# Attention with routed experts on one core: values and first sums of a group at step 5, and the low part of the row maxima between the two maxima of that step

## The reference

```python
x = x + attention(layernorm(x), ctx)          # kv = ctx @ Wkv.T, q = ln(x) @ Wq.T, causal softmax, @ Wout.T
x = x + ffn(layernorm(x))
# ffn: logits (T, 512, 8); probs = softmax; top 2 of 8, weights divided by their sum
#      final[t,o] = sum_e c[t,e] * (h @ expert_w[e].T + expert_b[e])[t,o]
#      with c[t,e] = sum over o of the weight that column o gives to e
```

## Time and profile before

| | |
|---|---|
| runs of the kernel before | 1996.59 us median of 3 (1994.41 to 1997.58) |
| the profiled execution, its own time | 1992.97 us |
| span of its profile | 1991.2 us |
| TensorE clock granted, whole span | 0.991 |
| PE busy | 1910.7 us, 96% |
| DVE busy | 1432.4 us, 72% |
| ACT busy | 1038.7 us, 52% |
| POOL busy | 858.1 us, 43% |
| chain that ended last, PE's share | 62% |

### The profile page before, as it was taken

The page is one execution under the profiler, slowest core; times in us unless marked ns, Lnnn a source line. Parts: engine busy times, 40 slices in busy tenths (PEclk is TensorE's granted clock), DMA queues, the critical chain, the costliest instruction groups (busy, mean ns, idle before and its releaser), DMA issues.

```text
span 1991.2 us, 30425 instructions
## 1 busy us (share of the span) xinstructions
PE 1910.7 (96%) x9772; PEld 1512.0 (76%) x9772; DVE 1432.4 (72%) x2840; ACT 1038.7 (52%) x2062; POOL 858.1 (43%) x1016
## 2 busy tenths in 40 slices
PE   4899999999997899999999999999999999999999
PEld 3666777777764788888888888788888888888887
DVE  5667767767666848787888888477777777777732
ACT  2566566566554347877777877533444333344400
POOL 5577777777676235455454435101321111132100
PEclk8999999999998999999999999999999999999999
DMA  5554555455465477786856455732232222223111
GB/s 165 122 127 127 134 143 134 123 143 138 106 176 197 158 243 239 242 269 222 253 211 232 168 207 195 285 111 79 82 125 89 79 87 92 79 83 124 51 42 32
DMA packets 103693, 294.54 MB, mean 148 GB/s; under 512 B 13777, under 2 KB 14801, under 8 KB 98482
## 3 DMA queue, kind: packets, MB, share of 16 engines
q1 hardware_dynamic: 91394, 209.44, 33.0%
q10 hardware_dynamic: 8880, 67.37, 10.5%
q0 software_dynamic: 3328, 16.78, 3.7%
HBM read 150.31 MB, written 109.16 MB: 130 GB/s over the span
## 4 chain that ended last, share of the span: by engine, by line
PE 62%; DMA 2%; DVE 2%; ACT 1%; issue 0%; SPq 0%; ACTq 0%; DVEq 0%
PE pair L261 20%; PE pair L263 20%; PE pair L262 20%; DMA w_raw<-w_fix 1%; PE ps L902 1%; DMA xb<-x 1%; DVE w_raw L1521 0%; DMA lg_all<-ev_c 0%; DVE w_raw L1525 0%; DVE w_l L1562 0%; ACT xb L1205 0%; ACT w_h L1200 0%; ACT w_h L995 0%; ACT ev_c L1223 0%; DVE tree L1580 0%
## 5 line engine op out<-in xcount | busy, mean ns | idle before, releaser
L261 PE MATMUL pair<-w_h,hT 128*128 128x512 f32 x1920 | 751.4, 391 | 6.7 <-ACT w_h L1200 3.7
L263 PE MATMUL pair<-w_h,hT 128*128 128x512 f32 x1920 | 747.8, 389 | 0.0
L262 PE MATMUL pair<-w_l,hT 128*128 128x512 f32 x1920 | 747.8, 389 | 0.0
L1904 POOL TENSOR_TENSOR logits<-logits,second 128x512 f32<-128x512 f32 x224 | 298.2, 1368 | 593.4 <-DVE second L1601 593.1
L261 PEld LDWEIGHTS pair<-w_h,hT 128*128 128x128 f32 x1920 | 360.8, 188 | 82.3 <-issue 6.2
L263 PEld LDWEIGHTS pair<-w_h,hT 128*128 128x128 f32 x1920 | 360.7, 188 | 75.8
L262 PEld LDWEIGHTS pair<-w_l,hT 128*128 128x128 f32 x1920 | 360.9, 188 | 74.0
L1704 DVE SCALAR_TENSOR_TENSOR xb<-pair,c_all,xb 128x512 f32<-128x512 f32 x256 | 191.8, 749 | 195.4 <-PE pair L263 189.0
L1095 ACT ACTIVATE pT<-pair,zero 128x1024 f32<-128x1024 f32 (+3 forms) x256 | 202.6, 792 | 204.6 <-PE pair L705 184.6
L1389 DVE CUSTOM_DVE_ANT_0 pair<-pair,future 128x256 f32<-128x256 f32 (+3 forms) x340 | 184.2, 554 | 124.2 <-PE pair L672 115.8
L1190 ACT ACTIVATE w<-tree 128x512 f32<-128x512 f32 x32 | 20.3, 635 | 387.5 <-DVE tree L1603 387.5
(11 more groups left out here) (166 smaller groups left out, 2607.3 us busy)
## 6 DMA issues: line engine op xcount, KB each, us to landing
logits<-lg_all ACTq DMA_DIRECT2D x32, 1792.0 KB, 8.9
qk_st<-qk SPq DMA_DIRECT2D x372, 128.0 KB, 2.4
lg_all<-ev_a SPq DMA_DIRECT2D x31, 768.0 KB, 8.4
lg_all<-ev_b SPq DMA_DIRECT2D x31, 768.0 KB, 4.7
xb<-x SPq DMA_DIRECT2D x64, 256.0 KB, 2.8
hT_all<-hT SPq DMA_DIRECT2D x32, 512.0 KB, 4.3
hT<-hT_all SPq DMA_DIRECT2D x32, 512.0 KB, 4.1
xt<-in_x SPq DMA_DIRECT2D x8, 1024.0 KB, 5.5
```

What stands on the lines that cost most here:

```text
L261: pe.matmul(dst, lh, rh, start=start, stop=False)
L262: pe.matmul(dst, lh, rl, start=False, stop=False)
L263: return pe.matmul(dst, ll, rh, start=False, stop=stop)
L1904: pool.tensor_tensor(logits[t % 2][:, e - 1, :], logits[t % 2][:, e - 1, :], second[:], ALU.subtract)\
```

## The change

It moves `first_sums`, the transposition of maxima, and `values_of(0)` and `values_of(1)` to step 5 in groups 0 to 2 (in group 3 they stay in step 7, with the sums first); `lo_shift` goes between the two maxima of step 5; the transposed maxima get other columns of their bank; SP sends the high row as soon as it is there, and `load_residual` and the last `store_sum` go behind the rows and the stack of heads. It spreads the projection's triples anew, and keys of group 3 go from step 5 to step 6 and to the other bank. Semaphore counts follow, and the second batch is written out ahead of the loop.

```diff
-        r_ps = d_ps[0:HC * QB, 0:P]
+        r_ps = d_ps[0:HC * QB, P:2 * P]
         def key_bank(c):
-            return 1 if c in (1, 2) else 0
+            return 1 if c else 0
         def key_step(c):
-            return 6 if c in (1, 2) else 5
-        OUT_FIRST = ((1, 0), (1, 6), (2, 3), (3, 0))
+            return 6 if c else 5
+        OUT_AT = (((1, 0), (1, 1), (1, 2), (1, 3)), ((1, 6), (1, 7), (2, 0), (2, 1)),
+                  ((2, 2), (2, 3), (2, 6), (2, 7)), ((3, 2), (3, 4), (3, 5), (3, 6)))
+        SUMMED_AT = ((1, 4), (2, 2), (3, 0), (3, 7))
         def key_rest(c):
-            return {0: (0, 5), 1: (1, 7), 2: (2, 7), 3: (3, 6)}[c]
+            return (c, 7 if c else 5)
...
@@ SP: rows(n, c)
-                sp.wait_ge(s["nm_hi"], n + 1)
-                sp.wait_ge(s["nm_lo"], n + 1)
-                for k, part in enumerate((nm_h, nm_l)):
+                for k, (part, name) in enumerate(((nm_h, "nm_hi"), (nm_l, "nm_lo"))):
+                    sp.wait_ge(s[name], n + 1)
@@ PE: body
                         shifted_scores(n, c, v, final)
+                        if v == TURN and c < KC - 1:
+                            next_scores(v)
+                            first_sums(n, False)
+                            turn_maxima(n + 1, c + 1)
+                            values_of(n, c, b, 0)
+                            values_of(n, c, b, 1)
+                            if out:
+                                project(v)
...
                         if v == key_step(c) and ahead:
                             take(key_bank(c), "K", n + AHEAD)
                             keys((c + AHEAD) % KC, b if c == 0 else b + 1, key_bank(c))
-                        if v == LAST and not final:
+                        if v == LAST and c == KC - 1 and not final:
+                            first_sums(n, True)
                             values_of(n, c, b, 0)
-                            first_sums(n, more or c < KC - 1)
                             values_of(n, c, b, 1)
@@ DVE: body
-                        if v == TURN + 1 and (more or c < KC - 1):
-                            lo_shift(n + 1)
...
+                            if v != TURN or masked(c, v):
+                                maxima(n + g, (c + g) % KC, vv, masked(c, v))
+                            else:
+                                maxima(n + g, (c + g) % KC, vv, heads=(0,))
+                        if v == TURN and (more or c < KC - 1):
+                            lo_shift(n + 1)
+                        if v == TURN and not masked(c, v) and (more or c + g < KC):
+                            maxima(n + g, (c + g) % KC, vv, heads=(1,))
```

More of the change, by code:

```diff
@@ L319, in out_block @@
         def out_block(c, v, last):
-            for i, (c0, v0) in enumerate(OUT_FIRST_LAST if last else OUT_FIRST):
+            if not last:
+                for i, steps in enumerate(OUT_AT):
+                    if (c, v) in steps:
+                        return i, steps.index((c, v))
+                return None
+            for i, (c0, v0) in enumerate(OUT_FIRST_LAST):
                 chunk = (c - c0) * UNITS + v - v0
@@ L327, in summed_block @@
         def summed_block(c, v, last):
-            step = c * UNITS + v - (0 if last else 1)
-            at = out_block(step // UNITS, step % UNITS, last)
+            if not last:
+                return SUMMED_AT.index((c, v)) if (c, v) in SUMMED_AT else None
+            at = out_block(c, v, last)
             return at[0] if at and at[1] == KC - 1 else None
@@ L823, in project, with project_query, next_scores @@
                         project_out(b - 1, i, chunk, 0)
+                    def project_query(v):
+                        if QUERY[v] == 0:
+                            take(1, "Q", n + AHEAD)
+                        queries(n + AHEAD, (c + AHEAD) % KC, QUERY[v])
+                    def next_scores(v):
+                        g, vv = target(c, v)
+                        if more or c + g < KC:
+                            if masked(c, v):
+                                scores(n + g, (c + g) % KC, vv, mask=True)
+                            else:
+                                scores(n + g, (c + g) % KC, vv, (0,))
                     def turn_tokens(i):
@@ L840, in body @@
                             values(VALUE[v])
[L841 to L844 removed]
+                        if v in QUERY and ahead and (c, v) != (1, 0):
+                            project_query(v)
+                        if v == SUMMED and out:
+                            project(v)
                         if v == SUMMED and not (first and c == 0):
@@ L858, in body @@
                                 turn_tokens(i)
-                        if out and not (c == 1 and v == 0):
+                        turning = v == TURN and c < KC - 1
+                        if out and not (c == 1 and v == 0) and v != SUMMED and not turning:
                             project(v)
-                        g, vv = target(c, v)
-                        if more or c + g < KC:
-                            if masked(c, v):
-                                scores(n + g, (c + g) % KC, vv, mask=True)
-                            else:
-                                scores(n + g, (c + g) % KC, vv, (0,))
-                        if v == TURN and (more or c < KC - 1):
+                        if not turning:
+                            next_scores(v)
+                        if (c, v) == (1, 0) and ahead:
+                            project_query(v)
+                        if v == TURN and more and c == KC - 1:
                             turn_maxima(n + 1, c + 1)
@@ L1371, in lo_of, with maxima @@
                     dve.tensor_tensor(qk[:, part], full[:], hi, ALU.subtract).then_inc(s["k_lo"], 1)
-            def maxima(n, c, v, mask=False):
+            def maxima(n, c, v, mask=False, heads=(0, 1)):
                 u = n * UNITS + v
                 i, pair = block_of(v), v % 2
-                if v == 0 and some(n - 1):
+                if v == 0 and 0 in heads and some(n - 1):
                     dve.wait_ge(s["turned"], n - 1)
@@ L1384, in maxima @@
                                       negate=True).then_inc(s["negmax"], 2)
-                for j in range(0 if mask else 2):
+                for j in () if mask else heads:
                     at = (2 * pair + j) * QB + i
```

41 lines of the change are left out of this document (22 added, 19 removed).

## The result

| | before | changed |
|---|---|---|
| median | 1995.74 us of 4 runs (1994.41 to 1997.58) | 2031.97 us of 4 runs (2029.61 to 2034.29) |
| ratio, 95% interval | | 1.0185 (1.0172 to 1.0197) |
| span of the profiled execution | 1991.2 us | 2030.5 us |
| clock granted, whole span | 0.991 | 0.983 |

The direction was right, the size was not: 2009 (1996 to 2018) was forecast. I read the same views of the changed kernel as of the one before. First the windows, a batch in the middle between two transpositions of maxima, and a stretch of the second batch. The columns are those of the earlier trace rows.

A forecast was written before the change was run, and what follows sets the result against it. PE was taken to bound the attention stage, busy 70.33 of 72.73 us a batch. Terms 10.4 + 2.1 + 0.8 + 1.4 = 14.7 us gave 2007.7 on the profiled time, 2011.3 on the median; forecast 2009, range 1996 to 2018.

The forecast's parts named there:

- +1.3 us a batch: Group 0: keys behind the values delay DVE's low part and maxima, so PE waits; +10.4 us over 8 batches.
- Nothing waited for the rows there, so this is worth nothing: Groups 1 and 2: the transposition and `lo_shift` come earlier, with no gain counted.
- I take 0: Transposition between column-tiled sums and values: no net cost counted, between −5 and +6 us over the stage.
- the 0.3 us a batch for `k_lo`: Groups 1 and 2, values gone from step 7: the next step 0's query waits some 0.3 us, counted once.
- The DMA queues and POOL end no wait of PE in the middle batches: Reading of the old kernel's middle-batch timelines; largest sum of PE's waits was on DVE's maxima.
- −1.3 us a batch: Group 3, steps 5 and 6: waits of 0.87 for maxima and 0.26 for the residual go, with 0.2 of restarts.
- +0.35 a batch: Projection spread and new waits in groups 1 to 3, +1.65, less group 3's 1.3; +2.1 us over 6 batches.
- +0.8: First batch: no projection fills steps 6 and 7, maxima hold up groups 1 and 2, group 3 gains 0.4.
- +1.4: Last batch: +0.5 at group 1, step 5, and some 0.9 us for router weights waiting behind `lo_shift`.
- The rival in which the last batch frees POOL: POOL's 10.61 us select gets in before DVE's later weights; up to 6.2 us back, 2000 to 2004; chance 0.15.

The follow-up runs named there:

- both repairs: On the changed kernel: group 0's keys right behind step 5's shifted scores, and keys' low part of groups 1 to 3 ahead of step 6's maxima; 2005.42 us, 1.0066.
- all values back and no spread: Changed kernel with values, sums and transposition back in all groups and the output projection's old spread; 1989.05 us, 0.9975.
- all values back: Changed kernel with values, first sums and transposition back in their old steps in all four groups, new projection spread kept; 1991.99 us, 0.9992.
- group 0 alone: On the version with both repairs: values, sums and transposition of groups 1 and 2 put back; 1990.47 us, 0.9987, and once more 1990.71 us, 0.9976.
- group 0 back, low part sooner: Changed kernel with group 0's values back in step 7 and keys' low part of groups 1 to 3 ahead of step 6's maxima; 2009.61 us, 1.0082.
- both repairs, last batch back: On the version with both repairs: values, sums and transposition put back in the last batch alone; 1999.99 us, 1.0039.
- group 0 alone, without the spread: On the version with group 0 alone: output projections of blocks 2 and 3 and their sums in their old steps; 1984.38 us, 0.9947.
- the last experiment: Changed kernel with only the output projections of blocks 2 and 3 and their sums back in their old steps; 2039.18 us, 1.0232.

## Why the forecast fell short, step by step

- **"+1.3 us a batch" in group 0:** right in mechanism, +1.73 in the trace. The term was put at 10.4. Moving the triple gave back 20.7 to 22.6 us, and putting the values of this group back 15.4 to 17.4. Eight times 1.73 would be 13.8; the rest is at half speed and in the irregular second and last batches, and was not separated further.
- **"Nothing waited for the rows there, so this is worth nothing", and "I take 0" for the tiles:** **this is the step that failed.** These are the terms of the move in groups 1 and 2, and beside them the sum has only the 0.3 us a batch for `k_lo`. Putting these two groups back gives 22.6 us with group 0 back too, 17.6 of it with the stack on time as well, and 15.0 in the version with both repairs. The runs name three parts of that. The stack comes late (next point): 5.0 of the 22.6. Each group moved costs 0.3 to 0.4 us a batch, of which the rows of PE place 0.19 to 0.25 at the transposition. And in the last batch PE meets the long wait for POOL: 7.6 of the 17.6 in the traces. The rest stays open.
- **"The DMA queues and POOL end no wait of PE in the middle batches":** true, and the wrong question. A queue that ends no wait before can end one as soon as work that stood between two of its uses is taken away. ACT's rounding of the queries waits for the stack, and between the keys and that rounding lay the 2 us of values. No term had it; its removal gave 4 to 10 us in three versions.
- **"I take 0, between −5 and +6 us over the stage", for the tiles:** the upper side was right. The rows show that a 128x16 transposition among 128x32 tiles costs 0.19 us, a little less than the 0.24 that I had worked out. The rule of the Trainium skill that I had weighed, "TensorEngine Tiling (Array Packing)", Key Properties, is that a change of mode drains the engine. The 0.19 agree with it; that draining is the reason no run shows.
- **"−1.3 us a batch" in group 3:** both waits are gone in the changed kernel (its shifted scores of step 5 take 0.29 to the projection, and step 6 has no wait). By the version with all values back and no spread it is worth 0.5 at most: with the keys gone from step 5, PE there waits 0.39 for a maximum that they had covered, which no term had.
- **The spread, "+0.35 a batch" net of group 3:** with all values back the middle batches are 0.41 to 0.46 us longer than before, so the number came, and by luck. The spread itself costs 0.8 to 0.9 a batch in the traces where 1.65 was counted, the saving is 0.5 instead of 1.3, and the two errors cancel. Over the program the spread costs 6.3 us in the version with group 0 alone and about 3 with all values back; in the changed kernel it gives 7 to 9. The price of an edit depended on which waits it stood among, and I had priced it alone.
- **"+0.8" for the first batch:** 3.9 by the trace, 2.5 of it between transpositions 1 and 2, in which group 0's late keys stand. Moving them did not bring it back (2.1 there); what does is putting back the values of that batch (0.6 at its end) or of groups 1 and 2 (0.7, and 2.2 in that version's second profile).
- **"+1.4" for the last batch:** 7.2 to the last transposition, 4.8 of it between the two in groups 0 and 1, with 6.8 us at half speed there. The rival in which the last batch frees POOL did not come; the select took 10.61 us again, as in the earlier trace rows, and PE waited for it longer than in the kernel before, which stands first here:

```profile
624.07 0.66 PE L721 MATMUL ps<-pT,v_sb 128*32 128x128 f32 x8 [8.16 <-POOL pT L1832]
```

```profile
659.07 0.65 PE L733 MATMUL ps<-pT,v_sb 128*32 128x128 f32 x8 [11.40 <-POOL pT L1871]
```

Below, POOL in the changed kernel and in the version with group 0 alone, and in the windows of the changed kernel DVE busy for all of PE's wait:

```profile
648.41 10.61 POOL L1871 TENSOR_SCALAR_AFFINE_SELECT pT<-pT 128x256 f32<-128x256 f32 x1
```

```profile
609.09 4.97 POOL L1874 TENSOR_SCALAR_AFFINE_SELECT pT<-pT 128x256 f32<-128x256 f32 x1
```

```profile
647.60:659.00 11.40, 0.07 (x4) 0.00 (x0) 11.40 (x13) 3.28 (x3) 11.40 (x2) 0.66 0.86 332
659.00:668.30 9.30, 9.02 (x45) 4.25 (x46) 3.04 (x4) 3.50 (x5) 3.29 (x4) 0.50 0.53 169
```

This wait divides the versions. From the last transposition to the last matmul of attention's projection it takes 43.4 to 45.3 us in the ten traces in which one select takes 10.6, the kernel before among them. It takes 37.1 to 37.5 in the six in which the slow select takes 4.97 to 4.99, and 35.8 to 36.0 in the three in which no select is slow and another instruction of POOL, the low part of the heads, takes 10.6 to 11.5 instead. Some of them (us):

```
                                       last transposition     from there to the
                                       to end of attention    end of the span
kernel before                          44.7                   1340.4
changed kernel                         45.0                   1344.6
group 0 back, low part sooner          43.6                   1345.1
all values back                        36.0                   1343.2
both repairs                           37.1                   1347.1
both repairs, last batch back          37.1                   1342.0
group 0 alone                          37.5                   1341.9
group 0 alone, without the spread      37.3                   1344.1
```

So the rival that I had given 0.15 is worth some 8 us, and it came in eight other versions and not in this one. Both traces of the changed kernel have the long select and both with group 0 alone have the short one; whether it belongs to the version or to the execution is not shown beyond that.

- **The clock was taken as it stood.** Of a span at a mean grant of 0.991, 36 us are at half speed (1991.2 x 0.009 x 2); of the changed one's, at 0.983, 69. The 33 more cost up to 16.5 us where PE sets the pace. The versions largely follow: 69 us in the slowest two, 60 with the keys of group 0 first (0.985), 44 with both repairs (0.989), 36 with group 0 alone (0.991); the fastest has 44. In three of the traces that I looked at closely the stretches stand behind waits: the last batch above, the second batch, and once per batch in the last experiment. So a part of what each repair gave may have come back through the clock. After the last transposition the changed kernel has 27 us at half speed and the one before 17; behind attention alone, where no line was changed, 10.5 against 3.4, which can make up to 3.6 of the 4.1 us that are lost there.

**What stays open:** why the medians of the version with both repairs and of the one with group 0 alone differ by 15.0 us. Their traces have 4.0 of it in the first batch (2.5 by the second profile), 4.6 in the next six, and 4.8 behind the last transposition (24 against 14 us at half speed). That waits of the last batch start the half-speed stretches behind it is what the windows suggest; no experiment changed the one without the other. Open too is what decides whether a POOL instruction of the last batch is held for 5 or for 10.6 us, and which one; no experiment moved DVE's rewriting of the weights, beside which it happens.

## What to carry to other kernels

When work is taken out from between two others, look at every engine's next use of what the two share, ACT's and the queues' too, and ask how long the transfers between them take; that they ended no wait before is no answer. Keep the instruction that heads another engine's in-order list (here the keys, one triple of 0.71 us) ahead of the work that is moved in: this alone was 21 to 23 of 36 us. And try the parts apart: of this change the keys of group 3 in step 6, the values of group 0 behind their keys and the keys' low part ahead of two maxima, without the spread and without groups 1 and 2, make the kernel 0.53% faster instead of 1.85% slower. Even then, see where the gain stands: in the trace of this version 2.3 us are won up to the last transposition, 7.4 from there to the end of attention, by the shorter wait for POOL, and 3.7 are lost behind it.

## What the runs showed of the hardware

Short waits of PE can stand ahead of a fall of the clock: a stretch with waits of 0.39 and 0.79 us within 2 us (PE busy for 5.61 of 6.80 us) was followed by 3.4 us at a granted clock of 0.50, four batches in a row. That the waits are the cause is not shown. A 128x16 transposition between runs of 128x32 tiles costs 0.19 us more than among untiled matmuls. Twelve transfers issued one after the other on SP took 7.82 us to issue, and ACT could start 1.9 us after the last of them.

One select of POOL with 128x256 elements, 0.41 us in the median, took 10.61 us while DVE was busy without a break (11.40 of 11.40 us, in 13 instructions); in five other versions the slowest took 4.97 to 4.99. "SBUF — State Buffer" in the Trainium skill, section "SBUF: two separate sides", says that on the port pair that DVE and POOL share the one that starts first has it for its whole instruction and the other is blocked, among others where DVE's instruction has two inputs in SBUF, as the rewriting of the weights has, and POOL's reads SBUF. The trace agrees that POOL stands while DVE works; that it stood through a whole row of DVE's instructions, none of them over 1.5 us, is what the trace shows beyond that.
